# Another order of the same blocks on all five engines of a two-layer attention and FFN kernel

## The reference

```python
x = x + attention(ctx, layernorm(x), mask)        # 8 heads of 16, keys ctx[:, :128], values ctx[:, 128:]
x = x + ffn(layernorm(x))                         # 128 -> 512 -> 512 -> 128, weights of +-1, relu
h = rmsnorm(layernorm(x)) @ W_in.T + b_in         # the depool layer
p = scan(rmsnorm(ctx)[..., :128])                 # s[t] = a*s[t-1] + u[t]
x = x + h + p[plug]                               # plug: cumsum of the patches' ends - 1, clipped
gates = softmax(layernorm(x) @ Wg.T + bg)         # 8 experts, the best 2
x = x + sum over the best 2 of gate * (layernorm(x) @ W[e].T + b[e])
```

## Time and profile before

| | us |
|---|---|
| median of 3 runs (530.83 to 535.12) | 530.94 |
| span of the profiled execution, first to last instruction | 529.3 |
| TensorE busy in that span | 489.3 |
| VectorE busy | 442.1 |
| ScalarE busy | 341.8 |
| GpSimd busy | 344.4 |

### The profile page before, as it was taken

How to read it: one execution, slowest core, us unless ns; L and a number is a source line. 1 busy time by engine, 2 the same in 40 slices (tenths; PEclk the granted TensorE clock), 3 DMA queues, 4 the chain that set the end, 5 groups by cost and what they waited for, 6 DMA issues and landing times.

```text
span 529.3 us, 14960 instructions
## 1 busy us (share of the span) xinstructions
PE 489.3 (92%) x5490; PEld 306.4 (58%) x5490; DVE 442.1 (84%) x1428; ACT 341.8 (65%) x732; POOL 344.4 (65%) x595
## 2 busy tenths in 40 slices
PE   3677989999999999999999999999999999999976
PEld 2663576656565666656665655656565566554443
DVE  7776678888898999888898989888889876779796
ACT  2546777877768667867787566768575767754311
POOL 6448114787685769878484947669667386567762
PEclk9976999999999999999999999999999999999988
DMA  7350212013041120140403021050102000000001
GB/s 214 106 159 26 77 42 62 32 46 102 21 112 36 44 80 1 32 122 2 115 2 96 1 77 48 25 144 28 46 3 77 27 1 2 27 1 22 0 20 41
DMA packets 14193, 28.04 MB, mean 53 GB/s; under 512 B 3656, under 2 KB 5032, under 8 KB 14120
## 3 DMA queue, kind: packets, MB, share of 16 engines
q1 hardware_dynamic: 13672, 26.60, 17.3%
q10 hardware_dynamic: 448, 0.48, 0.3%
HBM read 22.80 MB, written 4.24 MB: 51 GB/s over the span
## 4 chain that ended last, share of the span: by engine, by line
PE 46%; DVE 10%; issue 3%; POOL 1%; ACT 1%; DVEq 0%; POOLq 0%
PE ps L2354 12%; PE ps L2418 12%; PE ps L2247 3%; PE ps L2299 3%; PE ps L2365 3%; PE ps L2347 2%; PE ps L2316 2%; PE ps L2385 2%; PE ps L2386 2%; DVE weighed L1207 2%; DVE h L1129 2%; PE ps L2274 1%; DVE xo L1225 1%; PE ps L2324 1%; DVE pick L1099 1%
## 5 line engine op out<-in xcount | busy, mean ns | idle before, releaser
L2418 PE MATMUL ps<-w_T,y4T 128*128 128x512 f32 x256 | 125.9, 617 | 3.5 <-DVE weighed L1207 3.3
L2354 PE MATMUL ps<-h,w 128*128 128x512 f16 x512 | 120.1, 379 | 0.5 <-DVE h L1129 0.5
L1793 ACT ACTIVATE h<-ps 128x512 f16<-128x512 f32 x128 | 74.5, 593 | 59.6 <-PE ps L2354 45.5
L1129 DVE SCALAR_TENSOR_TENSOR h<-ps,h 128x512 f16<-128x512 f32 x128 | 85.9, 681 | 15.4 <-ACT h L1793 14.1
L711 POOL TENSOR_TENSOR sum<-weighed 128x512 f32<-128x512 f32 x59 | 75.3, 1277 | 27.6 <-DVE weighed L1207 27.6
L671 POOL TENSOR_TENSOR ve<-mv,eps 128x4 f32<-128x4 f32 x64 | 14.7, 230 | 110.2 <-DVE mv L1053 110.0
L1207 DVE TENSOR_TENSOR weighed<-ps,wgt 128x1024 f32<-128x1024 f32 x59 | 71.7, 1216 | 14.7 <-PE ps L2418 14.2
L2354 PEld LDWEIGHTS ps<-h,w 128*128 128x128 f16 x512 | 47.6, 98 | 58.1 <-issue 8.6
L1759 ACT ACTIVATE prT<-ps,maskT 77x1024 f32<-77x1024 f32 x64 | 67.4, 1102 | 15.7 <-PE ps L2303 15.7
L2418 PEld LDWEIGHTS ps<-w_T,y4T 128*128 128x128 f32 x256 | 45.3, 192 | 46.6 <-issue 35.5
L676 POOL TENSOR_TENSOR rs<-ve,neg_half 128x4 f32<-128x4 f32 x64 | 65.6, 1025 | 8.6
(11 more groups left out here) (157 smaller groups left out, 929.7 us busy)
## 6 DMA issues: line engine op xcount, KB each, us to landing
cx<-in_ctx SPq DMA_DIRECT2D x16, 320.0 KB, 4.5
vx<-in_values SPq DMA_DIRECT2D x16, 320.0 KB, 4.8
kT<-in_keys SPq DMA_DIRECT2D x16, 308.0 KB, 3.3
xa<-in_x SPq DMA_DIRECT2D x16, 256.0 KB, 2.9
out_x<-xo SPq DMA_DIRECT2D x16, 256.0 KB, 2.8
plugs<-plug_d SPq DMA_DIRECT2D x16, 77.0 KB
w_T<-in_weights SPq DMA_DIRECT2D x1, 592.0 KB, 4.2
weighed<-in_weights SPq DMA_DIRECT2D x1, 592.0 KB, 5.9
```

The costliest lines, as they stand in the source:

```text
L1129: last = nc.vector.scalar_tensor_tensor(h[:, 1, (k - 1) % FC, :], src, 0.0, h[:, 0, (k - 1) % FC, :], ALU.max, ALU.subtract)
L1793: last = nc.scalar.activation(h[:, 0, (k - 1) % FC, :], src, ACT.Relu)
L2354: last = pe.matmul(pb(g, k), w2[:, i, c * 128:(c + 1) * 128], h1[:, g.p, part, i, :], start=(i == 0 and part == 0), stop=(i == FC - 1 and ...
L2418: last = pe.matmul(pm(g, j)[:, half, :], y4T[:, g.p, j * S:(j + 1) * S], w_moeT[:, half * 512:(half + 1) * 512], start=True, stop=True)
```

## The change

All five lists are put in another order; a block does what it did. TensorE's list has fewer extra waits (768 rows before, 764 after), because in the new order most of them follow from waits that stand there anyway. The wait of `plug` for `plug_out` now holds for groups 0 and 1, since `plug(g[1])` comes first.

```diff
             def plug(g):

-                if g.n == 0:
+                if not g.has(2):
                     sp.wait_ge(plug_out, 32)
...
             load_rows(g[0])
             load_mask()
+            load_rows(g[1])
+            load_values(g[0])
             load_lens()
+            load_context(g[1])
+            load_keys(g[1])
...
-            a_turn_rows(g[5], (a_prT[1], g[3]))
...
+            a_turn_rows(g[5])
```

More of the change, by code:

```diff
@@ L1274, in _ @@
             b_low(g[0], 0)
+            a_stats(g[4])
             b_low(g[0], 1)
             b_low(g[0], 2)
+            a_picks(g[1])
             b_low(g[0], 3)
@@ L1355, in _ @@
             a_highest(g[6], 0)
+            a_picks(g[4])
+            b_low(g[3], 5)
             e_weigh(g[1], 3)
-            b_low(g[3], 5)
-            a_residual(g[4])
-            b_stats(g[4])
+            a_highest(g[6], 1)
             b_low(g[3], 6)
-            a_highest(g[6], 1)
+            a_stats(g[8])
+            a_split_maxima(g[6])
             b_low(g[3], 7)
@@ L1649, in _ @@
             d_stats(g[13])
+            a_picks(g[15])
             b_low(g[14], 8)
```

922 lines of the change are left out of this document (457 added, 465 removed).

## The result

The changed kernel takes 548.41 us (median of 4 runs, 547.43 to 551.72) where the kernel before took 530.88 beside it. The ratio is 1.032, with a 95% interval of 1.028 to 1.037: 3.2% slower. The prediction was 529.4 us in a range of 521.5 to 538.5, so it was wrong: a small gain was forecast (1.5 us), a loss of 17.5 us came, and it lies outside the range.

What follows compares the result with a forecast made beforehand. The prediction took TensorE to bound a long middle stretch between two chain-bound ends. From 529.3 us, -3.7, +1.2, +1.0 and 0 gave a 527.8 us span; the median, 1.6 above, was 529.4 us, range 521.5 to 538.5.

Steps and rivals of the forecast that it cites:

- What bounds the kernel: Whole kernel: a long stretch bound by TensorE between chain-bound ends; gains only from its 40.0 us idle or low-clock stretches.
- (a): Steady part: VectorE's split of the maxima leaves the place ahead of `c_turns` and `e_weigh`, removing TensorE's stalls; -3.7 us.
- Rival 2: Steady part: the stalls only move, as another two-input VectorE operation meets GpSimd; 531.9 us, chance 0.10.
- (b): Steady part: the split, now ahead of `d_gates` or `d_top`, can delay `e_experts(g, 0)`; +1.2 us, bounds 0 and 15.
- rival 4: Steady part: the split ahead of the gates delays `e_experts(g, 0)` in most groups; 536.2 us, up to 543.2, chance 0.18.
- (c): Steady part: `a_picks` and `a_stats` move a few places within a group, which comes back; nothing put down.
- The start, first half: Start: mask rows queue behind bulk loads, so the first scores start at about 16 us, 5.9 us later than before.
- The start, second half: Start: VectorE's work up to group 0's b statistics hides most of the late scores' delay; +1.0 us, bounds -3 and +5.9.
- rival 5: Start: the whole 5.9 us delay of the first scores is carried on; 534.3 us, chance 0.12.
- The end: Last groups: the wait for `e_weigh` goes and one for group 15's transposes replaces it; 0, between -1.5 and +1.5 us.

Runs made afterwards that it cites:

- x2: The kernel before with only VectorE's split of the maxima moved to right behind `d_gates` in nine groups; 533.6 us.
- t2: t1 with ScalarE's `b_high` of layers 6 and 7 moved ahead of `d_turned` in the same six groups; 537.7 us, ratio 1.012.
- s4: The kernel before with the changed kernel's first 15 SyncE calls and the signs' load first on ScalarE; 542.3 us, ratio 1.022.
- s2: The changed kernel with SyncE's first 12 calls put back in the order of the kernel before; 542.3 us.
- t1: s2 with TensorE's `d_turns` moved behind the next group's layer 7, and its gate blocks later, in six groups; 540.5 us.
- u3: s2 with VectorE's `b_stats` moved behind `d_stats` in groups 1 to 12, GpSimd's `rstd(ln_b)` and ScalarE's `b_normalise` following; 548.1 us.
- s5: s2 with VectorE's `make_plug` moved behind `a_stats(g[3])` and GpSimd's two `rstd` moved ahead of `a_patch_gain(g[0])`; 547.4 us.
- s6: s5 with GpSimd's `make_signs` moved ahead of the two `rstd` and VectorE's `make_weights` behind `b_stats(g[0])`; 546.5 us.
- s7b: s6 with ScalarE's `a_decays(g[0])` moved from ahead of `a_out_copy(g[0])` to behind it; 551.5 us.

## Why the prediction was wrong, step by step

- **What bounds the kernel.** Two chain-bound ends and a stretch bound by TensorE: right as a reading of before, and all three parts behaved as such. The conclusion that "a gain can only come from the 40.0 us in which TensorE is idle" left out its other half: a loss can come from anywhere, since every wait that costs nothing in the old order is a candidate in a new one. That is why both big terms were missing or far too small.
- **(a) The split leaves the e_weigh window, -3.7 us.** The waits named in the earlier trace rows did go, and the split is hardly stretched in the changed kernel (the longest operation of its four lines takes 0.44 us, where the earlier trace rows has 2.27). But x2, which makes this move alone, gained nothing: its waits are 6.1 us for 6.0. The step that failed is the equation of "the wait goes" with "the time goes". Rival 2, the stalls only move, described it (another operation with two SBUF inputs meets GpSimd's sum) and had a chance of 0.10. The lists were misread besides: before, the split stands between the second and third `e_weigh` only for groups 9, 10, 13 and 14, for 4, 8 and 12 it stood at the gates already, and group 12's moves into the window, not out of it.
- **(b) The split ahead of the gates, +1.2 us.** In the steady part no `e_experts(g, 0)` waits for `gd`; one does behind it, at 498.22, for 0.51 us. The cost is near 0, within the bounds, and rival 4 did not happen.
- **(c) "work that is only moved within a group comes back".** This is the step that failed in the steady part: nothing was put down for `a_picks` and `a_stats` on VectorE, `b_stats` is not named, and TensorE's own list and ScalarE's, where most of the loss can be given back, had no term at all. (The 768 and 764 given with the change do not count the extra waits: written out, TensorE's list has 221 before and 170 after.) Measured: +6.7 us, 5.7 of them given back by t2's two edits. What had to be read is in the old trace: 7.2 us of matmuls between `c_project` and `d_turns` against a chain of 6.3, 0.9 us of room. Both numbers changed, to 6.8 and 7.3.
- **The start, first half: scores at 16 us.** 21.88. The order was read rightly (all four mask rows are waited for, and SyncE's land last, 12.5 us behind their issue against 8.3 for ScalarE's), but the rate was not: 299 GB/s was taken from the densest window of before, and the changed kernel moved 222 GB/s over its first 20 us with the same engines full (0.95). The rows agree with what the prediction cites from the Trainium skill's "DMA: Bandwidth & Descriptors", section "Queues, rings and completion order": a queue's descriptors are consumed in ring order, and an engine takes turns between queues.
- **The start, second half: "VectorE is the one that is never free", +1.0 us.** It failed most: +13.1, far past the bound of 5.9. The walk assumed that other chains would hide the late scores, and summed VectorE's work without its waits. Its sum is short too: four blocks of 1.58, three of 1.45 and 7 us are 17.7, not "about 16", which would have made the term +2.8. s4 shows that a late SyncE list alone is carried to the end nearly whole (first scores +12.2, group 1 +11.5); rival 5 had the mechanism at 5.9 us. What s2 still has (5.6 us in its profile, 4.5 in the mean) shows as waits of one list for another, which the walk did not look for: it never asked what stands behind `make_plug` and `a_decays`, nor what stands ahead of `counts_out` in SyncE's list.
- **The clock.** The changed kernel is at the 1.2 GHz level from 53.4 to 70.4 us, with TensorE busy 14.9 of 17.0. The kernel before has 17.1 us at that level, in two pieces, busy 13.4. The stretch is as long, so it is not the main cause, but it lies in denser work: the same 420 matmul records are busy 35.7 us from 54 to 92 us (granted clock 0.78) and 32.7 us from 43 to 79 us of the kernel before (0.87). These are the 2 us that were added there.

```profile
53.40:70.40 17.00, 14.90 (x145) 10.02 (x149) 10.57 (x27) 11.00 (x26) 3.06 (x7) 0.50 0.10 30
```
- **The end.** 0 forecast, +0.7 measured, within its bounds and within the spread of the end; the wait for `weighed` was replaced by one for `xn`, as written.

Not settled: the last 4.5 to 5.6 us at the start, by block and by list (the other engines' or the rest of SyncE's), and why TensorE's records overlap less in the steady part.

## What to carry to other kernels

For a reordering, list for each block of the bounding engine how much of its own work lies between the producer's start and the block, and how long the chain over the other engines takes. Where the change makes the first shorter or the second longer by more than the room between them, expect a wait, even where the old trace has none. In this kernel a block moved on one engine gave little until the list of an engine around it moved too (t1 gave 1.0 us, t1 with ScalarE's list 5.7; u3, on VectorE with parts of GpSimd's and ScalarE's lists, lost 3.7), and a wait taken away was worth nothing in four runs (x2, s5, s6, s7b): another took its place each time. Name that one before counting the gain.

## What the hardware showed beyond what was expected

- With all 16 DMA engines taken (share 1.04 to 1.09) the rate was 210 GB/s in one window of 4 us and 284 and 295 in others of the same start. The busy share does not give the rate, and a landing time worked out from the best window comes out too early (16 us forecast, 21.9 measured).
- A small operation on VectorE from SBUF to SBUF can take as long as what GpSimd is doing beside it: `hit` 1.17 us and 0.25 us in the same run, and one operation of the split up to 2.27 us in the kernel before and never over 0.44 in the changed one. The 10 us of VectorE's time that this freed show nowhere in the kernel's time.
- A small transfer can pay for what was issued ahead of it in its queue: the 32 KB of the marks took 2.3 us when issued ahead of the weights and gains, and 9.2 us behind them, while these were still in flight.
